# Fused scan stages: a projection issued one lane sooner, guest work on other steps, first transfers in another order

## The reference, cut to what matters

```python
def step(h, inp):                       # layer 0: 4 directions, 384 channels; layer 1: 1 direction, 768
    dtt, ut, bt, ct = inp
    dA = jnp.exp(dtt[..., None] * A)
    h = h * dA + (dtt * ut)[..., None] * bt[:, :, None, :]
    y = jnp.einsum('bkdn,bkn->bkd', h, ct)
...
probs = jax.nn.softmax(scores, axis=-1)             # 4 experts, the best 2 kept and renormalized
h = jax.nn.gelu(jnp.einsum('bsd,edh->ebsh', x, w1) + b1[:, None, None, :], approximate=False)
y = jnp.einsum('ebsh,ehd->ebsd', h, w2) + b2[:, None, None, :]
out = jnp.einsum('bse,ebsd->bsd', masked, y)
```

## Time and profile before

| | us |
|---|---|
| median of 3 runs (lowest, highest) | 6015.15 (6009.82, 6017.5) |
| the profiled execution | 6005.91 |
| its span, first to last instruction | 6003.9 |
| mean granted TensorE clock | 0.904 of 2.4 GHz |
| the three image calls, first to last scan | 1325.0 to 2095.9, 2746.2 to 3515.9, 4162.1 to 4927.0 |
| the three shared calls | 2268.3 to 2645.9, 3688.1 to 4066.0, 5099.4 to 5475.3 |

### The profile page before, as it was taken

How to read it: one execution, slowest core, us unless ns; L and a number is a source line. 1 busy time by engine, 2 the same in 40 slices (tenths; PEclk the granted TensorE clock), 3 DMA queues, 4 the chain that set the end, 5 groups by cost and what they waited for, 6 DMA issues and landing times. The chain is left out here.

```text
span 6003.9 us, 66275 instructions
## 1 busy us (share of the span) xinstructions
PE 4872.5 (81%) x20263; PEld 3302.8 (55%) x20263; DVE 4680.5 (78%) x5015; ACT 3403.2 (57%) x5199; POOL 4056.8 (68%) x2861
## 2 busy tenths in 40 slices
PE   5767796778888896787888888777888888777998
PEld 2222242246666745555666645565666764554787
DVE  5999948958899848976999866895888984896544
ACT  3433353337777756655777755664777765664221
POOL 3999918938888817855888853883888871884221
PEclk8898898889999997888999998888999999788999
DMA  5555405437777605636777733553777760662110
GB/s 207 214 211 208 142 20 209 156 121 252 262 240 267 216 26 210 209 122 218 245 267 233 267 106 126 207 190 122 253 258 252 251 218 18 219 217 93 48 42 32
DMA packets 339174, 1076.86 MB, mean 179 GB/s; under 512 B 31378, under 2 KB 123122, under 8 KB 331128
## 3 DMA queue, kind: packets, MB, share of 16 engines
q1 hardware_dynamic: 338808, 1072.52, 51.6%
HBM read 1058.72 MB, written 13.68 MB: 179 GB/s over the span
## 5 line engine op out<-in xcount | busy, mean ns | idle before, releaser
L937 PE MATMUL banks<-ident,prod 128*128 128x128 f32 x4752 | 788.4, 294 | 614.4 <-DVE prod L1151 455.0
L937 PEld LDWEIGHTS banks<-ident,prod 128*128 128x128 f32 x4752 | 591.7, 150 | 861.7 <-DVE prod L1151 653.8
L1138 DVE TENSOR_TENSOR_SCAN banks<-banks,h 128x512 f32<-128x512 f32 x594 | 727.2, 1224 | 156.5 <-POOL h L1089 90.1
L476 PE MATMUL banks<-prod,ident 128*128 128x512 f32 x972 | 566.2, 723 | 300.7 <-DVE prod L618 233.3
L1089 POOL TENSOR_TENSOR h<-lane,Bb 128x512 f32<-128x512 f32 x576 | 722.9, 1273 | 84.8 <-DMA Bb<-half_rows 74.2
L1030 ACT ACTIVATE banks<-lane,A 128x512 f32<-128x512 f32 x864 | 579.5, 685 | 296.8 <-DVE half_delta_a L1119 103.6
L534 ACT ACTIVATE banks<-delta_first,A 128x1024 f32<-128x1024 f32 x288 | 321.8, 1118 | 579.6 <-DVE prod L618 480.1
L1151 DVE TENSOR_TENSOR prod<-banks,half_C_a 128x512 f32<-128x512 f32 x792 | 547.9, 692 | 114.8 <-DMA half_C_a<-half_rows 17.9
L1098 POOL TENSOR_TENSOR h<-h,half_C_a 128x512 f32<-128x512 f32 x360 | 462.4, 1284 | 245.7 <-DVE half_carry_a L1143 178.8
L476 PEld LDWEIGHTS banks<-prod,ident 128*128 128x128 f32 x972 | 196.2, 220 | 660.7 <-DVE prod L618 404.8
L971 PE MATMUL banks<-Cb,w_a 128*128 128x256 f32 x2304 | 556.9, 382 | 2.3 <-ACT Cb L1043 2.3
(11 more groups left out here) (382 smaller groups left out, 10994.3 us busy)
## 6 DMA issues: line engine op xcount, KB each, us to landing
Bb<-half_rows SPq DMA_DIRECT2D x576, 512.0 KB, 4.3
w_a<-w_in SPq DMA_DIRECT2D x256, 576.0 KB, 5.6
Cb<-half_rows SPq DMA_DIRECT2D x288, 512.0 KB, 4.6
half_C_a<-half_rows SPq DMA_DIRECT2D x160, 512.0 KB, 7.4
Bb<-rows SPq DMA_DIRECT2D x144, 512.0 KB, 4.2
Cb<-rows SPq DMA_DIRECT2D x144, 512.0 KB, 4.1
w_b<-w_in SPq DMA_DIRECT2D x128, 576.0 KB, 5.5
C_first<-rows SPq DMA_DIRECT2D x40, 1024.0 KB, 8.0
```

What stands on the lines that cost most here:

```text
L476: mm = eng.matmul(ps[:, c, :], m.ident[:, :], src[:, cols(c)], start=n == 0, stop=added(s) == (i + 1) * N, skip_group_check=True)
L937: mm = eng.matmul(ps[:, 0, at], src[:, at], m.ident[:, :], start=n == 0 and k == 0, stop=added(s) == (i + 1) * N, is_transpose=True, skip_ ...
L1138: eng.tensor_tensor_scan(flip(to), flip(slot(s)), flip(m.dBu[:, s % DRIVES, :]), initial, ALU.mult, ALU.add).then_inc(st.scanned, 1)
```

## The change

- The projection of a new group moves from the last lane of the group before to the lane before that (`fresh(i + 2)`): product after PE's step n = 8, `take_projection` at n = 11, the rows stored at n = 12. The delta of every lane now stands at n = 4 and `du` at n = 14. C is loaded at the same steps as before.
- The image call's pattern goes from ((1,8,9),(6,13,14),(11,18,20)) to ((2,8,9),(7,13,14),(12,19,21)): ups one step later, the third gelu at n = 3 instead of 2 of the next lane, the third pair of downs at n = 5 and 6 instead of 4 and 5. The shared call's pattern stays.
- An evict stands 3 steps behind the first `down` of its pair instead of 4. In the image call it stays at n = 8 (21 + 3 for 20 + 4), in the shared call it goes from n = 7 to n = 6.
- First transfers: `to_experts` already loads the first two B pairs of the image call and no longer waits for the gates' DMA. In `fused_scans` both C pairs and B come ahead of the weights, the semaphores of the stage before are cleared behind them, and the second weights, the reload of x and the load of w_out are issued at steps 1 to 9.
- The gates' row is loaded in four pieces of 512 KB at n = 2, 6, 10 and 14 of lane 1; the late row goes to lane 2.

```diff
--- before.py
+++ after.py
@@ -668,10 +668,10 @@
     STEPS = LANES * N
     SLOTS, DRIVES, PRODS, HELD, BRING = 4, 3, 3, 3, 3
     PAIRS = N // 2
-    PROJECT_AT, LOW_AT, STORE_AT = 3, 5, 6
-    COPY_AT, BACK_AT, TAKE_AT, SUM_AT = 3, 4, 7, 8
+    PROJECT_AT, LOW_AT, STORE_AT = 11, 11, 12
+    COPY_AT, BACK_AT, TAKE_AT, SUM_AT, DELTA_AT = 3, 4, 7, 8, 4
     BEHIND, KEEP = 2, 3
-    C_AT = {STORE_AT: (0,), 8: (1,), 9: (2,), 11: (3,), 13: (4,), 15: (5,)}
+    C_AT = {6: (0,), 8: (1,), 9: (2,), 11: (3,), 13: (4,), 15: (5,)}
     C_LATE = {1: (6,), 3: (7,)}
     PER = HT
     UNITS = len(guests) * E * PER
@@ -742,7 +742,7 @@
     gelus = {pair_at(v, 1): v for v in range(PAIRS_IN)}
     downs = {pair_at(v, 2) + k: 2 * v + k for v in range(PAIRS_IN) for k in range(2)}
 
-    evicts = {pair_at(v, 2) + 4: (v + 1) * 2 // PER - 1 for v in range(PAIRS_IN) if (v + 1) * 2 % PER == 0}
+    evicts = {pair_at(v, 2) + 3: (v + 1) * 2 // PER - 1 for v in range(PAIRS_IN) if (v + 1) * 2 % PER == 0}
     LAST = max([STEPS] + [s + 7 for s in evicts])
 
     def chunk(k):
@@ -754,15 +754,11 @@
     def hidden(u):
         return ps[:, 7, u % 2 * QUARTER:(u % 2 + 1) * QUARTER]
 
-    def delta_at(i):
-
-        return i * N + (10 if fresh(i + 1) else 4)
-
     places = [("projection", 0), ("delta", 0)]
     for step in range(STEPS):
-        if fresh(step // N + 1) and step % N == PROJECT_AT:
-            places.append(("projection", step // N + 1))
-        if step // N + 1 < LANES and step == delta_at(step // N):
+        if fresh(step // N + 2) and step % N == PROJECT_AT:
+            places.append(("projection", step // N + 2))
+        if step // N + 1 < LANES and step % N == DELTA_AT:
             places.append(("delta", step // N + 1))
         if step // N and step % N == SUM_AT:
             places.append(("sum", step // N - 1))
@@ -845,26 +841,16 @@
                     eng.wait_ge(moved.sent, 16 * (q + 1))
                     eng.dma_start(m.x[:, :, there], following[:, :, there]).then_inc(moved.reloaded, 16)
 
-            load_b(0)
+            if late is None:
+                load_b(0)
             load_c(0, 0)
-            load_b(1)
-            p.clear_last(eng, st)
-            if guests:
-                load_w1(0)
-                load_w2(0)
+            if late is None:
+                load_b(1)
             load_c(0, 1)
             load_b(2)
             if guests:
-                load_w1(1)
-                load_w2(1)
-            if late is not None:
-                eng.wait_ge(st.aside, 2)
-            if following is not None:
-                for there in range(len(guests) * QUARTER, L, QUARTER):
-                    at = slice(there, there + QUARTER)
-                    eng.dma_start(m.x[:, :, at], following[:, :, at]).then_inc(moved.reloaded, 16)
-            if load_ahead is not None:
-                load_ahead(eng, st.ahead)
+                load_w1(0)
+            p.clear_last(eng, st)
             for s in range(LAST + 8):
                 i, n = s // N, s % N
                 t = i // TILES
@@ -873,14 +859,31 @@
                         load_b(s // 2 + BRING)
                     if i == 0 and n % 2 == 0 and n // 2 + 2 < PAIRS:
                         load_c(0, n // 2 + 2)
-                    if late is not None and s == N:
-                        eng.dma_start(g.row[:, :, :].rearrange("p e l -> p (e l)"),
-                                      gates.to_broadcast([P, E * L])).then_inc(st.row, 16)
+                    if guests and s == 1:
+                        load_w2(0)
+                    if guests and s == 3:
+                        load_w1(1)
+                    if guests and s == 5:
+                        load_w2(1)
+                    if following is not None and s == 9:
+                        if late is not None:
+                            eng.wait_ge(st.aside, 2)
+                        for there in range(len(guests) * QUARTER, L, QUARTER):
+                            at = slice(there, there + QUARTER)
+                            eng.dma_start(m.x[:, :, at], following[:, :, at]).then_inc(moved.reloaded, 16)
+                    if load_ahead is not None and s == 9:
+                        load_ahead(eng, st.ahead)
+                    if late is not None and s == 1:
+                        eng.wait_ge(st.gates, 16)
+                    if late is not None and i == 1 and n % 4 == 2:
+                        e = n // 4
+                        eng.dma_start(g.row[:, e, :], gates[:, e * L:(e + 1) * L].to_broadcast([P, L])).then_inc(st.row, 16)
+                    if late is not None and i == 2 and n == 4:
                         eng.dma_start(late.row[:, :, :], gates.rearrange("o (e l) -> o e l", e=E)[:, :, L - QUARTER:L]
                                       .to_broadcast([P, E, QUARTER])).then_inc(st.late_row, 16)
+                    if fresh(i + 2) and n == STORE_AT:
+                        store_rows((i + 2) // TILES)
                     if fresh(i + 1):
-                        if n == STORE_AT:
-                            store_rows(t + 1)
                         for q in C_AT.get(n, ()):
                             load_c(t + 1, q)
                     if fresh(i) and i:
@@ -981,9 +984,9 @@
                         add(s - BEHIND)
                     if i and n == BACK_AT:
                         back(i - 1)
-                    if fresh(i + 1) and n == PROJECT_AT - 3:
-                        project(i + 1)
-                    if i + 1 < LANES and s == delta_at(i) - 4:
+                    if fresh(i + 2) and n == PROJECT_AT - 3:
+                        project(i + 2)
+                    if i + 1 < LANES and n == DELTA_AT - 4:
                         dt_product(i + 1)
                 if s == STEPS - 1:
                     back(LANES - 1)
@@ -1056,9 +1059,9 @@
                         eng.activation(ut[:, i, :].rearrange("p (w h) -> p w h", w=WW),
                                        u[:, i, :].rearrange("p (h w) -> p w h", w=WW),
                                        ACT.Copy).then_inc(st.turned, 1)
-                    if fresh(i + 1) and n == LOW_AT:
-                        take_projection(i + 1)
-                    if i + 1 < LANES and s == delta_at(i) + 1:
+                    if fresh(i + 2) and n == LOW_AT:
+                        take_projection(i + 2)
+                    if i + 1 < LANES and n == DELTA_AT + 1:
                         magnitude(i + 1)
                         exp_of(i + 1)
                         log_of(i + 1)
@@ -1106,7 +1109,7 @@
                 drive(s)
                 if n >= BEHIND and by_pool(s - BEHIND):
                     weigh(s - BEHIND)
-                if n == (15 if fresh(i + 1) else 14) and i + 1 < LANES:
+                if n == 14 and i + 1 < LANES:
                     du(i + 1)
 
         @block.vector
@@ -1161,7 +1164,7 @@
                 e = k % E
                 eng.wait_ge(st.down, (k + 1) * PER)
                 if late is not None:
-                    eng.wait_ge(st.row, 16)
+                    eng.wait_ge(st.row, 16 * min(k + 1, E))
                 if k:
                     eng.wait_ge(st.accumulated, k)
                 for f in range(CT):
@@ -1221,11 +1224,14 @@
             eng.dma_start(u, following).then_inc(st.fetched, 16)
             eng.wait_ge(first.st.low, 1)
             eng.dma_start(first.rows, first.low[0:BC, :]).then_inc(first.st.stored, 16)
+            eng.wait_ge(first.st.stored, 16)
+            for b in range(2):
+                pair = first.rows[2 * b:2 * b + 2, :].rearrange("(o r) l -> o (r l)", o=1)
+                eng.dma_start(m.Bb[:, b, :], pair.to_broadcast([P, L])).then_inc(first.st.b[b], 16)
             eng.wait_ge(st.taken, 1)
-            eng.dma_start(gates.rearrange("o (a n) -> (o a) n", n=P), r.turned[0:E * TT, :]).then_inc(st.kept, 16)
+            eng.dma_start(gates.rearrange("o (a n) -> (o a) n", n=P), r.turned[0:E * TT, :]).then_inc(first.st.gates, 16)
             if sent is not None:
                 eng.wait_ge(sent, 16)
-            eng.wait_ge(st.kept, 16)
 
         @block.tensor
         def _(eng):
@@ -2429,7 +2435,7 @@
                                         reverse=k >= 2, A=decay_0(k), dt_at=k * C, take=take) for k, take in order]
                     guests = [(slice(q, q + QUARTER), slice(q, q + QUARTER)) for q in range(0, L - QUARTER, QUARTER)]
                     fused_scans(p, half_scan_tensors(fused, name + "0"), g, s_scan, s_moved, directions, CT, half_rows, guests,
-                                ((1, 8, 9), (6, 13, 14), (11, 18, 20)), out, following=following, turn=(u, ut), late=late, gates=gates)
+                                ((2, 8, 9), (7, 13, 14), (12, 19, 21)), out, following=following, turn=(u, ut), late=late, gates=gates)
 
             def image(name, late, out, following):
```

(4 more changed lines are left out.)

## The result

| | before | after |
|---|---|---|
| median of 4 runs (lowest, highest) | 6012.48 (6007.67, 6017.5) | 5908.74 (5901.9, 5913.19) |
| ratio, 95% interval | | 0.9826 (0.9809 to 0.9843) |
| profiled execution, span | 6005.91, 6003.9 | 5910.61, 5908.1 |
| mean granted clock | 0.904 | 0.914 |
| six calls, first to last scan, summed | 3436.9 | 3344.7 |

The kernel is 104 us faster by the medians; 73 were forecast. The time of 5908.7 lies in the forecast's range of 5905 to 5992, but within 4 us of its lower end. Of the 95.8 us that the profiled span fell, 92.2 are in the six calls. Those of SP's loads are lower by 4: B is L809 and C is L818. B's buffers have the names Bb and Cb in the views, so a row of L809 that writes Cb is a load of B.

The account below looks back on a forecast made before the run. DVE was taken to bound the lanes, with gains only where lanes exceed their plain neighbours. Gains of 126.2 us less losses of 52.9 gave -73.3, from the median 6015.2 to 5942; range 5905 to 5992.

Parts of the forecast that it names:

- Projection out of the last lane: Image lanes 2, 8, 14, 20 lose their stalls, gain 54.0 us; lanes 5, 11, 17 gain 17.5.
- Projection into the lane before: Image lanes 1, 7, 13, 19: projection delays decays 12 and 14, 1.7 us a lane, 22.5 lost in all.
- PE starts its lane 0.8 earlier (below): Lane 13: PE's add of step 0 follows the copy of the sum, 0.8 us earlier than before the change.
- The two POOL waits of 0.4: Lane 13: POOL waits of 0.4 us at steps 14 and 15, which were to be absorbed.
- Gelu at n = 3: First halves of image calls: scan of step 4 comes 0.43 us late in 33 lanes, 14.2 lost.
- Lanes 4, 10, 16: Image lanes with an evict behind n = 8: projection there costs zero; without that cover 1.9 us each.
- Gates' row: Image lane 1: row loaded in pieces between the B loads, gain 10.0 us over three calls.
- Starts: Call starts: image first scan 2.4 us sooner, gain 7.2; image lane 0 gains 11.9, shared lane 0 gains 13.6.
- The rival with lanes 0 bound by bandwidth: Lane 0 runs its excess bytes at full rate whatever the order and gains nothing: 5967 us, chance 0.17.
- Shared call: Lane 0 gains 13.6 us, lane 5 gains 12.0; lane 4 loses 4.5, the evict in lanes 3 and 6 11.7.
- the one in which the losses don't show: Rival: PE catches up and gelu's block fits, so 22.5, 14.2 and 4.5 are not lost: 5901 us, chance 0.10.
- the stall moves whole: Rival: lanes 1, 7, 13, 19 lose 4.5 us each, 4, 10, 16 lose 1.9, likewise shared 4: 5998, chance 0.13.

Follow-up runs that it names:

- experiment 3: Changed kernel with the projection back in the group's last lane, new pattern kept: 5952.64 us.
- Experiments 1: Changed kernel with the image call's old pattern back and its evicts 4 behind the downs: 5957.87 us.
- experiment 2: Changed kernel with only the third gelu back at n = 2: 5947.72 us.
- the square: Table of image lanes 7, 13, 19; 2, 8, 14, 20; 5, 11, 17 summed: before 994.3, move alone 975.1, pattern alone 982.2, both 929.5 us.
- (10): Changed kernel with the gates' row in one DMA of 2 MB and the late row behind it, at step 16: 5915.31 us.
- (9): Changed kernel with the gates' row in one DMA of 2 MB at step 16, late row left in lane 2: 5916.74 us.
- experiment 8: Changed kernel with the first two B pairs loaded at the image call's start instead of ahead: 5918.05 us.
- (7): Changed kernel with semaphores, both weights, x and w_out again issued ahead of the second C pair and third B: 5935.84 us.
- Experiment 5: Changed kernel with the reload of x issued six steps later than the store of the finished quarter: 5900.02 us.

## Why the prediction was right, and where not

- **Projection out of the last lane: right.** -50.5 and -16.6 for -48.8 and -17.5. What the sum didn't have: 15.4 of the 50.5 need the new pattern. With the old one the move alone brings lanes 2, 8, 14, 20 from 437.6 to 402.5 only, since PE still starts them late. The sum also gives these lanes as 34.58 to 37.20 long, while the longest is 37.52, and it put PE's low clock (22.6 of its 54.0, experiment 3) down to the projection's place.
- **Projection into the lane before: the step that failed.** I gave these twelve lanes +22.5, and with gelu and row +17.7; they came out at -5.3. The nine without the row (7, 13, 19) came out at +2.3 for +21.3. The wrong term is "PE starts its lane 0.8 earlier (below)". The sum itself had the copy end where the block begins, at 1752.4, so begin at 1751.8, which is 1.8 earlier than 1753.65; I then wrote "1752.8 or so". Measured it is 1.7 (4.5 to 2.8 us into the lane). And I carried the lead through as a constant, which it isn't: the projection begins 17.6 us into the lane where my sum had 19.0 (1767.7 + 0.4 - 1749.1). So scan 14 waits 0.97 and not 1.8, and scan 12 not at all. Experiments 1 and 2 show that the copy's place does it: with the gelu at n = 2 the loss is there (396.2). DVE then waits 1.67 and 1.64 ahead of scans 12 and 14 in lane 7, close to what the sum had for 14. (The two POOL waits of 0.4 that the sum puts at steps 14 and 15 stand at step 15 and at step 0 of the next lane; both are gone after, as it had them. The 0.41 ahead of scan 9 it didn't have, and it was not traced.)
- **Gelu at n = 3: place and size right, sign wrong.** The wait is 0.46 for the forecast 0.43, in the 33 lanes. But I booked it as a loss of 14.2 with one benefit in passing; taken back alone it costs 39 us. It was the second half of the main gain, as the square and experiment 2 show. The drain that the Trainium skill has beside each table load (ScalarE: Activation LUTs, What ACT_TABLE_LOAD costs) shows here no more than it did before: the load at 1732.47, gelus at 1733.77, the second load at 1734.62 and the decay at 1735.92 stand 0.02 us apart.
- **Lanes 4, 10, 16: right**, +0.1. That it is the evict which covers the projection there was not tested by itself.
- **Gates' row: right in size, half wrong in cause.** Lane 1 took 9.9 more than lanes 7, 13 and 19 before, over three calls, and takes 1.4 more now: 8.5 of the 10.0. 5.6 of them come from keeping the two rows apart (10) and none from the pieces (9); the other 2.9 were not traced.
- **Starts: right.** -12.6 and -17.4 for 11.9 and 13.6, and by experiment 8 8.3 for 7.2 ahead of the calls. (The -3.6 in the table holds 4.7 that other stretches lost; each is 1 to 3 us, and they were not traced.) The rival with lanes 0 bound by bandwidth falls: the order alone is worth 32 us (7). The same bytes go either way (386 GB/s x 30.66 us is 11.8 MB, 326 x 36.01 is 11.7), at a DMA share of 1.00 now and 0.89 with the weights first: the full rate of the earlier trace rows had held for 20 us of 36 only. With the share at 1.00 the transfers may be what bounds lane 0 now; no run tests that.
- **Shared call: right but for the evict**, +5.3 for 11.7. The wait is there, 2.42 for 2.6 in lane 3, but lanes 3 and 6 lost 1.2 and 1.1 for the 1.95 each, and lane 9 gained 0.5. Part of the wait is made up within the lane, which the sum had no term for. Shared lane 4 is right in size (+5.2 for +4.5) only as far as a group that takes 94.0 to 96.9 from kernel to kernel can say.
- **Lane 9: not seen.** +9.0. It was covered by lane 8's stretch, which the change removes. The sum had asked what each moved step leaves behind, but not which load elsewhere had lived on the slack. Experiment 5 shows the cause.
- **The total** of the profiled spans is 22.5 better than the sum: 23.0 from lanes 1, 7, 13, 19 (the failed step, less 1.5 of the row), 6.4 from the evicts, 3.8 from shared lanes 0, 1.9 from smaller ones, less 9.0 for lane 9 and 3.6 outside the calls. The medians differ by 8 more, as the profiled execution before lay 6.6 below its median and the one after 1.9 above. The rival that came nearest is the one in which the losses don't show (5901), though the gelu's wait did show; "the stall moves whole" would have been nearer for lanes 1, 7, 13, 19 under the old pattern. That the time stayed in the range is partly luck: without the 9.0 of lane 9, which no term had, it would have been some 5900, below the lower end.

## What to carry to other kernels

Where engines run fixed lists in order, cost two moves together as well as apart: here the move alone gave 19 us, the pattern alone 12 and both 65, since one took a load off an engine's path and the other let that engine arrive in time. A step that lets a late engine start earlier is worth more than its own length if the engine's clock or backlog depends on that start; read its position at the moved step, not only at the lane's beginning. And when a stretch gets shorter, look for queues whose waits it had hidden: split "wait for the landing" from "issue" before that comes due.

## What was not expected of the hardware

- One gelu pair moved by one step on ACT changes PE's idle time at the start of lane 13 from 3.23 to 1.47 us, the span's mean granted clock from 0.904 to 0.914, and the whole kernel by 39 us. With the same 3.23 idle, a lane with 7 us at 1.2 GHz takes 33.4 us and one with 3 us takes 31.8.
- A store of 384 KB is known to have landed only 7.2 us after its issue, in a queue that loads keep busy.
- One broadcast of 2 MB and four of 512 KB cost the loads around them the same (94.1 and 93.9 us of lane 1); 512 KB more, at the same point, cost 1.9 us a lane.
